# Softmax sums of an attention layer taken on four 32-column tiles of TensorE instead of two 64-column ones

## The reference

```python
x = x + _layernorm(_L1_attn_ref(_layernorm(x), Wq, Wk, Wv, Wpost))
# _L1_attn_ref, 16 heads of 64:
raw_attn = jnp.einsum('bshe,bthe->bsth', Q, K * inv_sqrt_d)
attn = jax.nn.softmax(raw_attn, axis=2)            # over the keys t, no mask
A = jnp.einsum('bsth,bthe->bshe', attn, V)
A = jax.nn.gelu(A, approximate=False)
return X + A @ Wpost
...
x = x + _layernorm(_L1_ffn_ref(_layernorm(x), w_gate, w_up, w_down))   # silu(gate) * up, hidden 3072
```

## Time and profile before

| | us |
|---|---|
| median of 3 runs | 3648.88 |
| lowest, highest | 3481.66, 3765.32 |
| the profiled execution | 3484.66 |
| its span on the slowest core (core 0) | 3483.5 |
| spans of the eight cores | 3457.6 to 3483.5 |
| mean granted TensorE clock, by core | 0.965 to 0.969 |
| busy on core 0: TensorE / ScalarE / VectorE / GpSimd | 3162.8 / 1854.3 / 1514.3 / 648.2 |

### The profile page before, as it was taken

One profiled execution on the slowest core, in us unless ns is written; L12 is line 12 of the kernel. 1 busy time (PEld: TensorE's weight loads), 2 busy tenths in 40 slices (PEclk: granted clock), 3 DMA queues, 4 the chain that ended last, 5 costly groups with the idle time before them and its releaser, 6 DMA issues.

```text
span 3483.5 us, 50592 instructions; the slowest of 8 cores (3457.6 to 3483.5 us)
## 1 busy us (share of the span) xinstructions
PE 3162.8 (91%) x17670; PEld 1287.4 (37%) x17670; DVE 1514.3 (43%) x2452; ACT 1854.3 (53%) x1948; POOL 648.2 (19%) x1115
## 2 busy tenths in 40 slices
PE   5998886999999997779999999999999999999798
PEld 2444332443444432223333333333333333333333
DVE  2555565655665432243343343343344344344332
ACT  1443323333333327876676776676676676676421
POOL 1444433321223220010030030020020120120211
PEclk9999897999999999989999999999999999999999
DMA  7588747223332223623333343244243244243232
GB/s 163 128 186 165 188 110 166 95 86 91 103 106 82 82 100 97 154 91 125 114 128 116 108 138 119 95 138 128 92 137 127 88 138 132 87 139 113 74 116 94
DMA packets 192424, 412.79 MB, mean 118 GB/s; under 512 B 49584, under 2 KB 74160, under 8 KB 191024
## 3 DMA queue, kind: packets, MB, share of 16 engines
q1 hardware_dynamic: 180144, 369.70, 32.8%
q0 software_dynamic: 12032, 39.85, 8.0%
HBM read 357.06 MB, written 104.86 MB: 133 GB/s over the span
## 4 chain that ended last, share of the span: by engine, by line
PE 75%; DMA 7%; DVE 6%; ACT 6%; issue 4%; POOL 2%; DVEq 0%; SPq 0%; ACTq 0%; POOLq 0%
PE ps L1268 10%; PE ps L1316 10%; PE ps L1280 10%; PE ps L713 9%; PE ps L706 7%; PE p_t L1100 6%; PE ps L1081 6%; PE p_n L1103 5%; ACT c_pt L95 4%; PE ps L473 3%; PE ps L517 2%; PE p_n L417 2%; DMA a_wkT<-l_wkT 1%; DMA s_x<-r_xt 1%; DMA r_xa<-x 1%
## 5 line engine op out<-in xcount | busy, mean ns | idle before, releaser
L95 ACT ACTIVATE c_pt<-ps,negm 128x1024 bf16<-128x1024 f32 x1024 | 1075.7, 1111 | 230.1 <-PE ps L1083 229.1
L1100 PE MATMUL p_t<-c_pt,c_v 128*64 128x512 bf16 x2048 | 410.0, 397 | 5.1 <-DVE c_pvs L1114 4.6
L1081 PE MATMUL ps<-c_q,c_k 64*128 64x512 bf16 x1024 | 332.4, 386 | 83.8 <-ACT c_pt L95 72.7
L1103 PE MATMUL p_n<-c_pt,ones 128*64 128x512 bf16 x2048 | 398.4, 385 | 0.0
L1316 PE MATMUL ps<-c_wd,c_hh 128*128 128x512 bf16 x1536 | 351.4, 382 | 23.1 <-DVE c_o L1206 21.0
L1268 PE MATMUL ps<-c_h,c_wg 128*128 128x512 bf16 x1536 | 366.2, 381 | 1.2 <-DVE c_h L213 0.9
L1280 PE MATMUL ps<-c_h,c_wu 128*128 128x512 bf16 x1536 | 364.7, 380 | 0.0
L1083 PE MATMUL ps<-c_q,c_k 64*128 64x512 bf16 x1024 | 334.6, 389 | 0.0
L1274 DVE SCALAR_TENSOR_TENSOR c_th<-c_th,ps 128x512 f32<-128x512 f32 x192 | 132.1, 688 | 457.7 <-ACT c_th L95 457.7
L151 POOL TENSOR_SCALAR c_pof<-c_pof 128x1 f32<-128x1 f32 x32 | 6.6, 207 | 1440.0 <-DVE c_pof L144 1440.0
L95 ACT ACTIVATE c_th<-ps 128x512 f32<-128x512 f32 x192 | 114.6, 597 | 279.8 <-PE ps L1268 277.1
(11 more groups left out here) (191 smaller groups left out, 4353.8 us busy)
## 6 DMA issues: line engine op xcount, KB each, us to landing
c_wg<-s_wg SPq DMA_DIRECT2D x192, 256.0 KB, 2.8
c_wu<-s_wu SPq DMA_DIRECT2D x192, 256.0 KB, 3.2
s_x<-r_xt SPq DMA_DIRECT2D x64, 512.0 KB, 3.7
c_k<-s_k SPq DMA_DIRECT2D x64, 512.0 KB, 4.6
c_v<-s_v SPq DMA_DIRECT2D x64, 512.0 KB, 5.5
r_xa<-x SPq DMA_DIRECT2D x32, 512.0 KB, 8.7
r_xt<-x SPq DMA_DIRECT2D x32, 512.0 KB, 5.3
r_xa<-s_x SPq DMA_DIRECT2D x32, 512.0 KB, 5.4
```

Of the source, the lines that this page charges most:

```text
L95: return self.ACT.inc(self.nc.scalar.activation(*a, **k))
L1081: nc.tensor.matmul(bank[:, 0:512], k_[0:64, tc * 128:(tc + 1) * 128], q_[0:64, :], start=True, stop=True, tile_position=(0, 0))
L1100: nc.tensor.matmul(p_o[hd * 64:(hd + 1) * 64, :], v_[:, tc * 128 + hd * 64: tc * 128 + (hd + 1) * 64], p[:, hd * 512:(hd + 1) * 512], tile ...
L1103: ins = nc.tensor.matmul(p_l[hd * 64:(hd + 1) * 64, :], B.ones[:, 0:64], p[:, hd * 512:(hd + 1) * 512], tile_position=(0, hd * 64), **fl)
```

## The change

The block of ones becomes 32 columns wide. The 1024 exponentials of a key tile (head 0's 512 queries, then head 1's) are taken as four quarters of 256, and each quarter's sums are accumulated by a matmul of its own on another quarter of the array's columns: 32 partitions of `p_n` by 256 columns. So `p_n` then holds head 0's queries 0 to 255 in partitions 0 to 31, its queries 256 to 511 in 32 to 63, and head 1's in 64 to 95 and 96 to 127.

`finish` copies 256 columns instead of 512 to a new tile `c_rows`, takes the reciprocal in two pieces of 128 columns (due at 2.5 and 4.5), and then `place` (one call for each head, due at 6.5 and 8.5) copies the four 32x256 blocks that the head's 64 partitions by 512 columns of `c_sums` consist of: each half twice, once for each 32 of the 64 partitions. The product at 10.5 is as before. Eight such copies are made for a job.

```diff
+        self.rows = B.sb("c_rows", 256, F32)
...
-            for hd in range(2):
-                ins = nc.tensor.matmul(p_l[hd * 64:(hd + 1) * 64, :], B.ones[:, 0:64],
-                                       p[:, hd * 512:(hd + 1) * 512], tile_position=(0, hd * 64), **fl)
+            for qd in range(4):
+                ins = nc.tensor.matmul(p_l[qd * 32:(qd + 1) * 32, 0:256], B.ones[:, 0:32],
+                                       p[:, qd * 256:(qd + 1) * 256], tile_position=(0, qd * 32), **fl)
...
-            t_s = DVE.inc(v.tensor_copy(self.sums[:], p_l))
+            t_s = DVE.inc(v.tensor_copy(self.rows[:], p_l[:, 0:256]))
...
             def piece(q4):
                 DVE.wait(t_s)
-                DVE.inc(v.reciprocal(self.sums[:, q4 * 128:(q4 + 1) * 128], self.sums[:, q4 * 128:(q4 + 1) * 128]))
+                part = self.rows[:, q4 * 128:(q4 + 1) * 128]
+                DVE.inc(v.reciprocal(part, part))
+
+            def place(hd):
+
+                DVE.wait(DVE.tok())
+                for half in range(2):
+                    src = self.rows[hd * 64 + half * 32: hd * 64 + half * 32 + 32, :]
+                    for r in range(2):
+                        DVE.inc(v.tensor_copy(self.sums[hd * 64 + r * 32: hd * 64 + r * 32 + 32,
+                                                        half * 256:(half + 1) * 256], src))
...
-            for q4 in range(4):
-                B.after(2.5 + 2.0 * q4, lambda q4=q4: piece(q4))
+            for k2 in range(2):
+                B.after(2.5 + 2.0 * k2, lambda k2=k2: piece(k2))
+                B.after(6.5 + 2.0 * k2, lambda k2=k2: place(k2))
             B.after(10.5, last)
```

## The result

The changed kernel took 2.15% longer: ratio 1.0215, 95% interval 1.0191 to 1.0238. Its undisturbed executions lie at 3554.8, 3556.3 and 3562.4 us, those of the kernel before at 3481.5 to 3486.2; the medians of all runs (3674.7 and 3486.2) can't be set against each other, since other executions of either kernel ran with a lower granted clock on part of the chip. The forecast for such an execution was 3530 us (+1.3%), in a range of 3390 to 3580. The sign was right and the size fell short: +70 us on the profiled execution where +45 was forecast. The interval lies on both sides of the 2% line, so it doesn't decide between "slower", which had been given 0.26, and "the same", 0.57.

What follows compares the result with a forecast made beforehand. TensorE was taken to bound the interleaved part, ScalarE the first part; +46 us for shape changes less halved columns, VectorE zero, -1 for the shorter copy: +45 on 3484.7, so 3530 us (+1.3%), range 3390 to 3580.

Steps and rivals of the forecast that it cites:

- second rival: TensorE sums: four column tiles go two by two, slot stays 0.216 us; about 3617 us, +3.8%; chance 0.10.
- Changes between 64 and 32 columns are charged: TensorE, value and sums matmuls: three added shape changes per step cost 0.095 us each plus longer first matmuls.
- first rival: TensorE: changes between 64 and 32 columns are free, 0.216 us saved per step; about 3397 us, -2.5%; chance 0.23.
- The price of a change: TensorE step: 0.285 us for three changes plus longer first matmuls, 0.33 in all, less 0.216 gained: +0.114 us.
- 377 to 426 steps, +46: Interleaved part: +0.114 us in each step, up to 49 absorbed by exponential waits: +43 to +49 us, taken as +46.
- VectorE at zero, +/-5: VectorE's shorter copy, two reciprocals and eight added copies: -1.05 to +1.3 us per job, no effect on the end.
- only the output projection feels VectorE: TensorE's waits on VectorE: 9.2 us in 6 waits, a 0.8 us delay at each giving 5 us at most.
- waits for exponentials shrink somewhat: Sign on TensorE, 1560 to 3256 us: these waits shrink somewhat, but grow if the shape changes are free.
- The -1 for the shorter copy ahead of p_t: VectorE's 256-wide copy, 0.265 us shorter, shrinks TensorE's 8 waits, 4.6 us, by 2 at most: -1 us.
- The first part hidden: Attention running nearly alone, 64 steps: the added 0.114 us is hidden by TensorE's waits; without that cover 7 us.
- The clock: Rival, first part: halved sums lower TensorE's granted clock, 35 us on top, 3565 us; chance 0.04.
- The free case: TensorE without charge for 64-to-32-column changes: -81 to -92 us over 377 to 426 steps, -2.5%; chance 0.23.

Runs made afterwards that it cites:

- E6: Changed kernel with 128 instead of 256 columns in each of the four sums matmuls, leaving out half the sums: ratio 1.0076, interleaved part 1792.0 us.
- E1: Changed kernel with both value pairs of a step ahead of both groups of sums: ratio 0.9946, interleaved part 1744.7 us.
- E13: Changed kernel, values first, copies on GpSimd, sums of four key tiles together from job 8, six exponential tiles, two gate/up weight buffers: ratio 0.9795, 3430.1 us.
- E5: Kernel before, its 64-column sums kept, with both value pairs of a step ahead of both pairs of sums: ratio 0.9985, interleaved part 1761.6 us.
- E2: Changed kernel with TensorE's sums as in the kernel before, so VectorE's part alone; half the queries' sums left out: ratio 1.0026, interleaved part 1777.3 us.
- E8: Changed kernel with its eight 32x256 copies on GpSimd instead of VectorE: ratio 1.0150, interleaved part 1815.3 us.
- E4: Changed kernel issuing only two of the four 32-column sums matmuls: ratio 1.0171, interleaved part 1825.8 us.
- E10: Changed kernel with the eight copies in four calls of two instead of two calls of four: interleaved part 1831.0 us, by profile alone.
- E3: Changed kernel with sums as two matmuls of 64 columns by 256 queries, leaving out half the queries: ratio 0.9794, interleaved part 1704.7 us.

## Why the prediction was right or wrong

**Four tiles stream together: right.** The "x4" row and E6's slope say so. The second rival falls. The Trainium skill, "TensorE: Matmul & The Clock Gate", Part 3, has a packed group take one matmul and about 4 ns for each further tile, from which the prediction had estimated 0.12 us. The groups of four start 0.120 us apart in E1 and 0.109 to 0.120 in E13 (x16), which agrees within 0.01.

**Changes between 64 and 32 columns are charged: right, and this decided the sign.** The first rival falls by E1 against E5. The Trainium skill, "TensorEngine Tiling (Array Packing)", section Tiling Modes, lists 128x64 and 128x32 as two configurations and has a change of mode drain TensorE. The trace agrees in that the change costs: 0.34 us from values to sums where it was 0.24. The page has no figure for it.

**The price of a change was somewhat too low.** The sum took 0.285 plus 0.044 for three added changes, +0.114 a step. The step's distances (values to sums, to values, to sums, to the next shape) are 0.337, 0.223, 0.337, 0.226 on the median, 1.123, where they were 0.24, 0.216, 0.216 and 0.315, 0.987: +0.136. Leaving the 32-column group costs 0.223 - 0.108 = 0.115 where 0.095 plus 0.010 was taken, twice a step. So the period of a step went from 3.36 to 3.50, where 3.47 was forecast. Times 377 to 426 steps that is 51 to 58 us, and the term "377 to 426 steps, +46" measures 52 to 54, by E2 and E8: the count of steps was right.

**VectorE at zero, +/-5: the step that failed most.** It measures 14 to 16 us of the 25 that were missing. Two things in it were wrong. The first is the price "between 132 and 424 ns" for every copy: the usual copy, 284 ns, is inside, but 13 of 512 lasted 1.8 to 2.5 us, until GpSimd's addition had ended. The second is "only the output projection feels VectorE". TensorE's waits for that, 9.2 us in 6 waits, are the same in E2. I had looked for cover at TensorE's banks alone, 3.3 us of slack, and not at who else takes VectorE's results. ScalarE waits for the norm statistics, by way of GpSimd, and the exponentials stand behind in its queue. The kernel before had a row of that kind, c_h waiting for c_pre. Of the signs, "waits for exponentials shrink somewhat" told of it: in the interleaved part they grew from 49.2 to 52.9 us, mean of the cores, and shrank, to 45.3, only when the copies had left VectorE (E8). The sign named as "wrong outright", VectorE ahead of L1268 or L1280, didn't appear, since the delay took another way.

The -1 for the shorter copy ahead of p_t came true: TensorE's waits for it in the first part went from 3.7 to 2.3 us, mean of the cores.

**The first part hidden: wrong, by 4.6 us.** The average wait of 0.46 us was read as slack of the step. In the timeline of that part, the scores that show a wait are those of the odd key tiles; those of the even ones come right behind the weigh block, with no wait to show and hardly any slack. The changed kernel, core 0:

```profile
1453.17 0.37 PE L1082 MATMUL ps<-c_q,c_k 64*128 64x512 bf16 x1 [0.35 <-ACT c_pt L95]
...
1454.38 0.29 PE L1104 MATMUL p_n<-c_pt,ones 128*32 128x256 bf16 x4
1454.61 0.39 PE L1082 MATMUL ps<-c_q,c_k 64*128 64x512 bf16 x1
...
1455.18 0.37 PE L1082 MATMUL ps<-c_q,c_k 64*128 64x512 bf16 x1 [0.18 <-ACT c_pt L95]
...
1457.36 0.37 PE L1082 MATMUL ps<-c_q,c_k 64*128 64x512 bf16 x1 [0.35 <-ACT c_pt L95]
```

Steps of 2.01 and 2.18 alternate, where the kernel before has 2.01 and 2.06:

```profile
1455.13 0.37 PE L1081 MATMUL ps<-c_q,c_k 64*128 64x512 bf16 x1 [0.31 <-ACT c_pt L95]
1457.19 0.37 PE L1081 MATMUL ps<-c_q,c_k 64*128 64x512 bf16 x1 [0.36 <-ACT c_pt L95]
```

That is 0.06 a step, 4 us in 64 steps. With the shorter block of E1 the part is back at 165.7, and with TensorE's part as before (E2) at 165.3, while it is 169 to 171 in E4, E8 and E10, which change shape as often as the changed kernel. So it is TensorE's order and not VectorE. It comes near the 7 us that the prediction named for the case that the cover is gone.

**The clock: right to give it little.** Granted clock in the interleaved part stays at 0.98 to 0.99. By the granted clock of the stretches, the changed kernel is at the lower level for 11 to 30 us more than the kernel before between the first exponential and the second GELU. E1 has 12 to 27 us more and is no longer there than the kernel before, so no time is put down to it. But E1's steps are shorter, so this doesn't rule out a few us: of the 68 us of the interleaved part 11.6 lie before the second GELU, where an even share would be 9.

**The free case was overpriced.** It was put at 81 to 92 us; E3 against E2 gives 72.6 in the interleaved part, and the whole, with VectorE's 16 against it, is -2.1% by E3's ratio (between -2.6% and -1.5%), not -2.5%.

Sum as measured: TensorE 52 to 54, VectorE 14 to 16, first part 4.6, and -3 in layer 0 and after, where nothing was changed: 70 us.

## What to carry to other kernels

Halving the columns of a small matmul is worth only what is left after the changes of tile shape that it brings: here 0.108 us gained against about 0.1 to 0.12 lost at each change, so count the changes in the order of issue first and group matmuls of one shape. When work moves onto an engine with idle time, look in its queue and in the queues of all that consume its results, not only at the bounding engine's waits; here a half busy VectorE delayed ScalarE, and ScalarE delayed TensorE. Look too at what other engines do when the new instructions run, and at the smallest, median and largest time of a group, not at its mean: 331 ns on the mean were 284 ns, and some 2 us for the 13 copies beside GpSimd's additions. Before a row of waits is taken as a cause, compare it with the same instruction before the change, since the releaser that it names can be another than the one that held it. And a wait in a profile shows the slack of the instruction that waits, not of its neighbour that is late without waiting.

## What the runs showed of the hardware

- A change between 128x64 and 128x32 tiles costs about as much as the 0.095 us between whole and split columns or split rows: 0.10 us into the 32-column group, 0.115 out of it (E6: 0.117 independent of the columns).
- Four column tiles of 256 columns stream in the slot of one: inside a group of the same shape the next four start 0.11 to 0.12 us later (E1, E13); two such tiles instead of four save 0.006 (E4).
- A copy of 32x256 fp32 within SBUF took 284 ns on VectorE and 393 ns on GpSimd (E8). The 128x256 copy out of PSUM took 422 ns on VectorE; partitions and source both differ, so the difference isn't put down to either.
- Such a copy on VectorE that started during GpSimd's addition of 128x1024 fp32 elements in SBUF ended only 0.14 to 0.15 us after that addition, up to 2.5 us after its own start, in all 104 cases of the changed kernel's eight cores, and as often in E1, E2 and E10. The product L1136, which reads two SBUF tiles, was held in the same way once on each core (2.5 us, usually 0.69). Reciprocals of 128x128, norm statistics and additions that read PSUM kept their times beside the same additions (before: 0.90 us, 0.69 and 0.63).
